# Experts' outputs kept by token: an indirect store by POOL and plain loads, in place of stores by slot and indirect loads

## What is computed

```python
probs = softmax(x @ gate_w + gate_b)            # layer 0; layer 1 alike, on an rms-normed x
top_probs, top_idx = top_k(probs, 2)
top_probs = top_probs / sum(top_probs)
out = sum over e of dispatch[:, e] * ((silu(x @ w1[e]) * (x @ w2[e])) @ w3[e])
x = x + out
```

## Time and profile before

| | us |
|---|---|
| median of three runs (lowest, highest) | 1306.82 (1302.99, 1307.1) |
| the profiled execution | 1309.22 |
| its span in the trace | 1307.3 |

### The profile page before, as it was taken

How to read it: one execution, slowest core, us unless ns; L and a number is a source line. 1 busy time by engine, 2 the same in 40 slices (tenths; PEclk the granted TensorE clock), 3 DMA queues, 4 the chain that set the end, 5 groups by cost and what they waited for, 6 DMA issues and landing times.

```text
span 1307.3 us, 19647 instructions
## 1 busy us (share of the span) xinstructions
PE 967.6 (74%) x6816; PEld 838.2 (64%) x6816; DVE 770.5 (59%) x1800; ACT 468.5 (36%) x786; POOL 475.8 (36%) x371
## 2 busy tenths in 40 slices
PE   4758996788887888706724999944892893799992
PEld 2547885687787778506714888843582683688881
DVE  6637487776768677758675444314798656333322
ACT  2352648457676766125411111101360160111110
POOL 1537888877878777500001222222000000211103
PEclk9878998799999999856856999986896896799996
DMA  9861322222222222156204888861000001667662
GB/s 285 231 178 41 71 62 70 59 56 59 56 71 53 56 55 42 25 139 167 64 20 152 291 270 296 301 242 43 1 1 1 1 2 28 248 234 269 229 232 68
DMA packets 57580, 155.86 MB, mean 119 GB/s; under 512 B 23309, under 2 KB 33474, under 8 KB 49130
## 3 DMA queue, kind: packets, MB, share of 16 engines
q1 hardware_dynamic: 26414, 125.47, 29.2%
q0 software_dynamic: 25056, 24.10, 8.4%
q10 hardware_dynamic: 6048, 5.51, 1.2%
HBM read 133.82 MB, written 20.89 MB: 118 GB/s over the span
## 4 chain that ended last, share of the span: by engine, by line
PE 35%; DMA 21%; DVE 16%; issue 13%; POOL 13%; ACT 1%; POOLq 0%; SPq 0%; DVEq 0%; ACTq 0%
PE bank L683 12%; DMA pair_scores<-sc_ring,idx_ring 11%; POOL arena L1704 6%; PE bank L694 6%; POOL pair_scores L1714 5%; DMA arena<-row_tab,ids 5%; PE bank L631 4%; PE bank L420 3%; PE bank L430 2%; PE bank L620 2%; DMA arena<-pair_scores 2%; POOL arena L1769 2%; PE bank L748 1%; DMA arena<-xl_tab,idx_ring 1%; PE bank L468 1%
## 5 line engine op out<-in xcount | busy, mean ns | idle before, releaser
L1759 POOL DMA_INDIRECT arena<-row_tab,ids x42 | 58.7, 1397 | 597.5 <-DVE ids L1294 528.0
L1714 POOL DMA_INDIRECT pair_scores<-sc_ring,idx_ring x160 | 216.8, 1355 | 90.5 <-issue 52.3
L683 PE MATMUL bank<-arena 128*128 128x128 f32 (+1 forms) x1616 | 200.0, 281 | 0.0
L683 PEld LDWEIGHTS bank<-arena 128*128 128x128 f32 (+1 forms) x1616 | 188.0, 190 | 7.8 <-issue 3.6
L1704 POOL DMA_INDIRECT arena<-xl_tab,idx_ring x120 | 167.3, 1394 | 69.4 <-issue 32.6
L1306 DVE TENSOR_TENSOR arena<-bank,arena 128x512 f32<-128x512 f32 (+2 forms) x76 | 37.2, 508 | 157.0 <-ACT arena L1597 157.0
L694 PE MATMUL bank<-arena 128*128 128x256 f32 (+1 forms) x404 | 99.0, 388 | 0.0
L1497 ACT ACTIVATE late_ohT<-arena 125x875 fp32r<-125x875 f32 x100 | 90.6, 927 | 0.0
L446 PE MATMUL bank<-tab 125*128 125x314 bf16 x400 | 66.1, 319 | 30.8 <-DVE tab L902 30.8
L1597 ACT ACTIVATE arena<-bank 128x512 f32<-128x512 f32 (+2 forms) x76 | 32.4, 450 | 152.1 <-PE bank L683 152.1
L468 PE MATMUL bank<-late_hi,late_ohT 125*125 125x256 f32 x500 | 84.4, 300 | 0.5 <-DVE arena L868 0.5
(11 more groups left out here) (302 smaller groups left out, 1947.8 us busy)
## 6 DMA issues: line engine op xcount, KB each, us to landing
arena<-in_exp SPq DMA_DIRECT2D x25, 1024.0 KB, 6.1
arena<-in_exp SPq DMA_DIRECT2D x17, 1364.0 KB
arena<-in_exp0o SPq DMA_DIRECT2D x25, 512.0 KB, 5.6
pair_scores<-cnt SPq DMA_DIRECT2D x10, 1093.8 KB
arena<-pair_scores SPq DMA_DIRECT2D x10, 1093.8 KB
arena<-in_exp1o SPq DMA_DIRECT2D x17, 640.0 KB
slot_y<-arena ACTq DMA_DIRECT2D x42, 128.0 KB, 5.1
fa<-in_rows SPq DMA_DIRECT2D x10, 437.5 KB
```

The costliest lines, as they stand in the source:

```text
L683: mm = pe.matmul(banks[1 + 2 * q + buf][0:rows, i * SLOTS:(i + 1) * SLOTS], w_in(s, q, k, m, rows), xsT[:, s, k, :], start=(k == 0), stop= ...
L1714: p.indirect_dma_start(out=pair_scores[which], in_=sc_ring[:, b % 2, j, :], in_offset=None, out_offset=bass.IndirectOffsetOnAxis(ap=idx_ri ...
L1759: p.indirect_dma_start(out=xs[:, s, :], out_offset=None, in_=tab, in_offset=bass.IndirectOffsetOnAxis(ap=ids[:, s, :], axis=0))\
```

## The change

The results are kept by pair and not by slot. A new HBM table `y_tab` has 1 + 1250 rows: row 0 takes the results of empty slots, row 1 + 625 j + n that of choice j of token n. `node_id` gets a second column with these row numbers, so the same PE product `row_nodes` gives both numbers, and DVE `node_ids` keeps the second in `all_ids`. DVE `copy_y` copies the row numbers of its block to `rows_y` ahead of the result. POOL's new `scatter_y` writes `ys` to `y_tab` with one indirect DMA per block in place of ACT's plain store; in POOL's program it stands three blocks behind, after `gather_rows(b)` comes `scatter_y(b - 3)`. It waits for both copies of its block and for the landing of the previous scatter, since all scatters count on one semaphore. `copy_y(b)` waits for the scatter of b - 2. The ten indirect loads go; SP's `load_back` waits for all scatters and loads `yg` in three groups of tiles (0; 1 and 2; 3 and 4), each as four plain DMAs (two choices, partitions 0 to 111 and 112 to 124), twelve in all. `sloti` goes.

```diff
+BACK = [(0, 1), (1, 3), (3, T)]
+BACK_OF = [0, 1, 1, 2, 2]
...
-        slot_y = nc.dram_tensor("slot_y", [NBLK0 * SLOTS, D], F32).ap()
+        y_tab = nc.dram_tensor("y_tab", [1 + 2 * N, D], F32).ap()
...
-                    after(pe, sem(name + "_ycopied"), b - 1)
+                    after(pe, sem(name + "_ycopied"), b * 2 - 2)
...
                 def node_ids(b, s):
                     dve.wait_ge(sem(name + "_nodes"), b + 1)
                     after(dve, sem(name + "_turned"), b - 1)
+                    v.tensor_copy(all_ids[:, bass.ds(b, 1), :], banks[7][:, 1:2].unsqueeze(1))\
+                        .then_inc(sem(name + "_all"), 1)
                     v.tensor_copy(ids[:, s, :], banks[7][:, 0:1]).then_inc(sem(name + "_ids"), 1)
...
                 def copy_y(b, s):
                     dve.wait_ge(sem(name + "_out"), b + 1)
                     if not (isinstance(b, int) and b < 2):
-                        dve.wait_ge(sem(f"{name}_stored{s}"), (b - s) * 8)
+                        dve.wait_ge(sem(name + "_stored"), b * 16 - 16)
+                    dve.wait_ge(sem(name + "_all"), b + 1)
+                    v.tensor_copy(rows_y[:, s, :], all_ids[:, bass.ds(b, 1), :].rearrange("p a c -> p (a c)"))\
+                        .then_inc(sem(name + "_ycopied"), 1)
                     v.tensor_copy(ys[:, s, :], banks[5 + s][:, 0:D]).then_inc(sem(name + "_ycopied"), 1)
...
-                def store(b, s):
-                    act.wait_ge(sem(name + "_ycopied"), b + 1)
-                    act.dma_start(slot_y[bass.ds(b * SLOTS, SLOTS), :], ys[:, s, :])\
-                        .then_inc(sem(f"{name}_stored{s}"), 16)
...
+                def scatter_y(b, s):
+
+                    pool.wait_ge(sem(name + "_ycopied"), b * 2 + 2)
+                    if not (isinstance(b, int) and b == 0):
+                        pool.wait_ge(sem(name + "_stored"), b * 16)
+                    pool.sem_inc(sem("pool_turn"), 1)
+                    p.indirect_dma_start(out=y_tab, in_=ys[:, s, :], in_offset=None,
+                                         out_offset=bass.IndirectOffsetOnAxis(ap=rows_y[:, s, :], axis=0))\
+                        .then_inc(sem(name + "_stored"), 16)
+
+                def step(b, s):
+                    gather_rows(b, s)
+                    if not (isinstance(b, int) and b < 3):
+                        scatter_y(b - 3, 1 - s)
+
                 pool.wait_ge(sem(name + "_tab"), 16 * len(PARTS))
-                block_steps(pool, nblk, gather_rows)
-                for s in range(2):
-                    pool.wait_ge(sem(f"{name}_stored{s}"), 16 * ((nblk + 1 - s) // 2))
-                for t in range(T):
-                    for j in range(2):
-                        p.indirect_dma_start(out=yg[:, j, t, :], out_offset=None, in_=slot_y,
-                                             in_offset=bass.IndirectOffsetOnAxis(ap=sloti[:, j, t:t + 1], axis=0))\
-                            .then_inc(sem(f"back{t}"), 16)
+                block_steps(pool, nblk, step)
+                for b in range(nblk - 3, nblk):
+                    scatter_y(b, b % 2)
...
+            def load_back(name, nblk):
+                sp.wait_ge(sem(name + "_stored"), 16 * nblk)
+                for g, (a, b) in enumerate(BACK):
+                    for rows in PARTS:
+                        for j in range(2):
+                            tab = y_tab[1 + j * N + a * P:1 + j * N + b * P, :].rearrange("(t p) d -> p t d", p=P)
+                            sp.dma_start(yg[rows, j, a:b, :], tab[rows]).then_inc(sem(f"back{g}"), 16)
...
             sp.dma_start(vec[:, 0:V_SIZE], vec1_in.partition_broadcast(128)).then_inc(sem("vec1_in"), 16)
+            load_back("e0", NBLK0)
             sp.wait_ge(sem("e0_added"), 2 * T)
...
             expert_weights("e1", NBLK1, 2, exp1_in, [exp1o_in, exp1r_in])
+            load_back("e1", NBLK1)
```

More of the change, by code:

```diff
@@ L217, in build @@
         nblocks_i, bown_i = sb("nblocks_i", [P, NE0], I32), sb("bown_i", [P, NBLK0], I32)
-        slotf, sloti = sb("slotf", [P, 2, T]), sb("sloti", [P, 2, T], I32)
+        slotf = sb("slotf", [P, 2, T])
         before = sb("before", [P, P], BF16)
@@ L224, in build @@
         iota_s = sb("iota_s", [P, SLOTS], FP16)
-        node_id = sb("node_id", [P, T, 2], FP16)
+        node_id = sb("node_id", [P, 2 * T, 2], FP16)
         slot_rel = sb("slot_rel", [P, 2 * T])
-        ids = sb("ids", [SLOTS, 2, 1], I32)
+        ids, rows_y = sb("ids", [SLOTS, 2, 1], I32), sb("rows_y", [SLOTS, 2, 1], I32)
+        all_ids = sb("all_ids", [SLOTS, NBLK0, 1], I32)
         gpart, gate = sb("gpart", [P, 3, T]), sb("gate", [P, T])
@@ L661, in row_nodes @@
                     for q in range(2 * T):
-                        mm = pe.matmul(banks[7][:, 0:2], sel[:, s, q, :], node_id[:, q % T, :], start=(q == 0),
+                        mm = pe.matmul(banks[7][:, 0:2], sel[:, s, q, :], node_id[:, q, :], start=(q == 0),
                                        stop=(q == 2 * T - 1))
@@ L981, in _ @@
                 v.tensor_copy(xlr[:, t, :], bank[0:P, :]).then_inc(freed, 1)
-            dve.wait_ge(sem("iotas"), 5)
+            dve.wait_ge(sem("iotas"), 6)
             v.tensor_scalar(node_neg[:, :], node_f[:, :], -1.0, None, ALU.mult).then_inc(sem("node_neg"), 1)
@@ L1270, in route @@
                     own.link(v.tensor_reduce(slotf[:, j, :], pick[:, j, :, :], AX.X, ALU.add))
-                own.note(v.tensor_copy(slot_rel[:, :], slotf[:, :, :].rearrange("p j t -> p (j t)")))
-                v.tensor_copy(sloti[:, :, :], slotf[:, :, :]).then_inc(sem(name + "_routed"), 1)
-                own.fence()
+                v.tensor_copy(slot_rel[:, :], slotf[:, :, :].rearrange("p j t -> p (j t)"))\
+                    .then_inc(sem(name + "_routed"), 1)
+                dve.wait_ge(sem(name + "_routed"), 3)
             def experts(name, nblk, units, then):
@@ L1327, in experts @@
                 for t in range(T):
-                    dve.wait_ge(sem(f"back{t}"), 2 * 16 * (1 + int(name[1])))
+                    dve.wait_ge(sem(f"back{BACK_OF[t]}"), 2 * 16 * len(PARTS) * (1 + int(name[1])))
                     for j in range(2):
@@ L1600, in step @@
                         ins.then_inc(sem(name + "_silu"), 1)
-                    if not (static and b == 0):
-                        store(b - 1, 1 - s)
                 copy_turned(0, 0)
                 block_steps(act, nblk, step)
-                store(nblk - 1, (nblk - 1) % 2)
             def four_groups(g, segment):
@@ L1671, in _ @@
                    allow_small_or_imprecise_dtypes=True).then_inc(sem("iotas"), 1)
-            p.iota(node_id[:, :, :], pattern=[[P, T], [0, 2]], base=0, channel_multiplier=1,
-                   allow_small_or_imprecise_dtypes=True).then_inc(sem("iotas"), 1)
+            for w in range(2):
+                p.iota(node_id[:, :, w].rearrange("p (j t) -> p j t", j=2), pattern=[[w * N, 2], [P, T]], base=w,
+                       channel_multiplier=1, allow_small_or_imprecise_dtypes=True).then_inc(sem("iotas"), 1)
             p.iota(iota_e[:, :], pattern=[[1, NE0]], base=0, channel_multiplier=0,
```

## The result

The changed kernel takes 1341.1 us (median of four runs, 1334.5 to 1346.3) against 1305.7 of the kernel before: 1.027 times as long, 95% interval 1.022 to 1.032. The forecast was 1299.3, so both its sign and its range were wrong. The profiled execution took 1346.3 us, the longest of the four; its span is 1344.5 against 1307.3.

What follows compares the result with a forecast made beforehand. No single engine bounds the kernel: layer 0's blocks have PE with the gather on the path's edge, layer 1's PE alone. Blocks +5, ends -5.5 and -7 give -7.5: 1306.8 to 1299.3 us, range 1290 to 1317.

Steps and rivals of the forecast that it cites:

- The reading of before: Layer 0: gather on the edge of the path; layer 1: PE alone the limit; layer ends: savings count whole.
- The gather's start: Layer 0 blocks: behind the scatter on POOL, the gather starts 3.3 us after an output ends, 1.8 us later than before.
- The gather's issue: Layer 0 blocks: issued after DVE's compare has ended, it takes about 0.96 us instead of 1.38.
- The landing: Layer 0 blocks: the later gather meets only the burst's end and lands in 4.0 us, bounds 3.0 and 4.8.
- The rule of two steps: Layer 0 blocks: two steps take 5.73 + 3.3 + 4.0 = 13.0 us, 6.5 a step against 6.36; +5 us in all.
- Layer 1: Layer 1 blocks: the same delay needs 16.6 us for two steps that take 18.9, so no cost.
- The ends: After each layer's blocks: last scatters plus twelve plain loads replace ten gathers; -5.5 us in layer 0, -7 in layer 1.
- B: Layer 0 blocks: contention stays, gather lands in 4.8 us or more behind the scatter in one queue; about 1309; chance 0.20.
- C: Layer 0 blocks: late-landing scatters block POOL; at 8 us each the step is 8.3, net +30, 1335; chance 0.13.
- A: Layer 0 blocks: gather lands in 3.0 to 3.5 us, blocks gain or cost nothing; about 1293; chance 0.15.
- D: Layer ends: slower loads and lone scatters make each end 4 to 5 us later; net +1, about 1308; chance 0.10.

Runs made afterwards that it cites:

- experiment 4: Kernel before, no scatter, but POOL writes a scratch tile (about 2.3 us) ahead of each layer 0 gather from the fourth on; 1367.7 us.
- experiment 3: Changed kernel, but layer 0's weights after the second block loaded only in their first 128 columns; 1292.5 us.
- experiment 6: Changed kernel, but empty slots write distinct spare rows of y_tab instead of shared row 0, results right; 1330.2 us, ratio 1.018.
- experiment 7: Kernel of experiment 6 with landed scatters counted per buffer, so POOL waits for no previous scatter; 1329.8 us, ratio 1.019.
- x1_lag4: Changed kernel with the scatter four blocks behind the gather instead of three, so the gather is issued first; 1302.6 us, ratio 0.996.
- x11_loads_left: Kernel of experiment 7 with the scatter four blocks behind the gather, SP's large loads left in place; 1295.1 us, ratio 0.992.

## Why the prediction was wrong

*The reading of before* held: the gather was on the edge of layer 0's path, PE alone bounded layer 1, and the ends were saved whole.

*The gather's start.* 3.3 us after the output was forecast, 3.5 and 3.7 in turn were measured. Most of the 0.4 us is the scatter's issue, 1.72 us where 1.4 was taken from the gathers. The traces show why: such an issue beside the compare ends 0.82 to 0.87 us after the compare, whenever it began. The scatter began 0.62 us into the compare (783.54 against 782.92, compare until 784.40, issue until 785.26), the gathers of before mostly 0.84 to 0.94 us into it. The step was right in kind.

*The gather's issue* fell to 0.97 us, as forecast from the earlier trace rows.

*The landing* is the step that failed. "A gather that starts 1.8 us later meets only the end of the burst" looked at the burst of one block and took 4.0 us; it took today's median of 4.8 as the upper bound, though the earlier trace rows has landings up to 6.9. But SP issues the next block's first weights 1.6 us before the next output ends (786.12 against 787.67), and in a short step that is 4.3 us after this output. A gather issued at 3.7 us, 0.6 us ahead of that load, still meets it and lands only when most of it is through: 6.5 us here, 5.0 to 6.6 for the gathers issued like this one in the stretch. In the timed case of experiment 4 it lands 1.0 us after the load. What lands together in the earlier trace rows was the end of a burst; the prediction did not ask where the next one began. Experiments 3 and 4 show both halves: no weights, no late landing; a delay and no scatter, the same late landings.

*The step.* The rule of two steps was right and was filled with one mean landing. The traces show two kinds of blocks in turn: a short step bunches the weights of two blocks, the gather between them is late, the long step that follows lets the DMA engines drain (SP issues no weights between 787.85 and 797.66), the next gather is early and of no use. With the measured terms the rule gives 5.7 + 3.7 + 6.5 = 15.9 for two steps.

*The clock* was not in the sum at all. The missing 1.5 us of 17.4 is PE after its idle time. The multiplies of the hidden layer took 84.0 us before and 95.9 after, for the same 704:

```profile
712.10:852.50 140.40, 84.00 (x704) 82.00 (x704) 0.99 0.85 287
```

```profile
718.97:901.22 182.25, 95.94 (x704) 94.75 (x704) 0.91 0.65 221
```

That is 12 of the 42 us. In the experiments it goes with the idle time: 0.88 at a stretch of 196.5 us, 0.94 at 161.7, 0.99 at 145.5, 1.00 at 138.4.

*Layer 1* came out at no cost, by the argument given: its two steps of 18.9 us had room.

*The ends.* Layer 1: -7 forecast, -6.2 measured; a lone scatter of empty slots took 3.1 us (3.4 taken), and the first group of loads came 2.9 us after SP began (3.3 forecast), but the second 5.9 us after SP began, where 4.9 was forecast (1288.1 to 1293.0). Layer 0: -5.5 forecast, -4.5 measured. There the last copy waited for a scatter that landed beside the large loads; the prediction had hidden such landings up to 11 us behind two whole steps, but the last steps of the loop are short.

*The rivals.* B named contention and priced it at +12 to +17 in the blocks, with the cause in the shared queue; the queue was cleared by experiments 3 and 4, and the blocks lost 42. C had the size of the result (+30, a step of 8.3 us, and 182.3 / 22 is 8.3), but that is luck: its mechanism, POOL held by scatters that land late, accounts at most for the 7 to 9 us of the stretch by which the versions without such waits are faster (experiments 6 and 7). C was right that the shared row makes scatters slower, by 0.7 us for one alone. A's fast landing came too, 3.6 us, but in every second block, where nothing waits for it. D's slower ends took 2 us of the forecast and not 8 to 10.

## What to carry to other kernels

When an in-order engine that issues DMAs gets a second task, ask which of the two becomes ready at the same moment and which one is on the path, and put that one first; here one block more of lag for the stores was worth 37 us. A DMA on the edge of the path is not delayed by its own delay alone: look where the next large transfers begin, since the nearer it comes to them, the more it waits for them too. And an idle time of PE of some microseconds has to be priced with the slower multiplies that follow it.

## What the runs showed of the hardware

- A gather of 128 rows of 1 KB took 2.8 to 3.9 us to land beside light traffic (DMA share 0.23) and up to 6.9 us beside weights, with or without scatters in its queue (6.9 in the kernel before, 6.8 in experiments 4 and 7).
- Within the blocks the issue of such a DMA by POOL took 0.94 to 0.99 us, and 1.1 to 1.8 when it began while DVE's compare of 125 x 1280 in fp16 ran, for scatters and gathers alike: it then ended 0.82 to 0.87 us after the compare in all 20 cases of the kernel before, and in the changed kernel too. Two issues in `x1_lag4` that began 0.08 us ahead of a compare took 0.98 us. So an issue looks held until the compare is over. The Trainium skill (SBUF — State Buffer, "SBUF: two separate sides") names a port that DVE and GpSimd share as a cause; no run here separated that from other causes.
- After 4.2 us of idle time PE's granted clock was 0.50 for 2 us and averaged 0.69 over 5 us, and 32 multiplies took 4.93 us instead of 3.74.
- One scatter alone whose 128 rows were all the same row of HBM landed in 3.1 us, and in 2.4 us when the rows were distinct. Beside the weights the two were not separated: in `x1_lag4` POOL, held for a scatter's landing, went on up to 9.1 us after its start (788.19 to 797.28), where the slowest scatter with distinct rows took 6.8 us (`x11_loads_left`), but the two were not issued at the same point of the burst.
